# A graph network layer stack on one core: two looped slots in the adjacency build, and four basis chunks moved to the ends of tiles 9 and 11 of the first layer

## Time and profile before

| | us |
|---|---|
| median of 3 runs | 1826.44 (1819.98 to 1828.72) |
| the profiled execution | 1818.69 |
| its span, first to last instruction | 1816.4 |
| TensorE busy | 1754.4 (97%) |
| VectorE busy | 874.3 (48%) |
| ScalarE busy | 593.8 (33%) |
| build, about | 22 to 321 us of the span |
| first layer, tiles 0 to 11 | about 454 to 596 us |

### The profile page before, as it was taken

How to read it: one execution, slowest core, us unless ns; L and a number is a source line. 1 busy time by engine, 2 the same in 40 slices (tenths; PEclk the granted TensorE clock), 3 DMA queues, 4 the chain that set the end, 5 groups by cost and what they waited for, 6 DMA issues and landing times.

```text
span 1816.4 us, 22290 instructions
## 1 busy us (share of the span) xinstructions
PE 1754.4 (97%) x7318; PEld 849.3 (47%) x7318; DVE 874.3 (48%) x1889; ACT 593.8 (33%) x1232; POOL 10.8 (1%) x36
## 2 busy tenths in 40 slices
PE   5989888999999999999999999999999999999998
PEld 3555555433334444444444444444544444444444
DVE  7888887489885321112222224334253443594123
ACT  1555544466876311222110001232323323232000
POOL 1000000000000000000000000000000000000000
PEclk9999999999999999999999999999999999999999
DMA  7999989810302401000011116300000010021111
GB/s 176 247 288 280 247 235 245 318 36 2 144 24 82 168 4 43 0 1 23 0 47 35 35 35 241 147 0 30 1 0 30 1 41 1 1 82 58 35 47 47
DMA packets 45781, 157.80 MB, mean 87 GB/s; under 512 B 7686, under 2 KB 9630, under 8 KB 37094
## 3 DMA queue, kind: packets, MB, share of 16 engines
q1 hardware_dynamic: 43792, 146.95, 26.6%
q10 hardware_dynamic: 1878, 9.44, 1.4%
HBM read 120.71 MB, written 35.65 MB: 86 GB/s over the span
## 4 chain that ended last, share of the span: by engine, by line
PE 83%; DVE 6%; DMA 5%; issue 3%; DVEq 2%; ACT 1%; POOL 0%; POOLq 0%; ACTq 0%
PE psum L1549 31%; PE psum L1563 31%; PE psum L1790 7%; DMA hs<-in_L_gnn_basis 4%; PE psum L1477 2%; PE psum L1444 2%; PE psum L1740 2%; PE psum L1637 2%; PE psum L1624 1%; PE psum L1476 1%; PE psum L1515 1%; DMA adj<-in_L_gnn_basis 1%; DVE hs L716 1%; DVEq L695 1%; PE psum L1716 1%
## 5 line engine op out<-in xcount | busy, mean ns | idle before, releaser
L1563 PE MATMUL psum<-hs,adj 128*128 128x512 f16 x2880 | 636.3, 380 | 0.0
L1549 PE MATMUL psum<-wb,xt 128*128 128x512 f32 x1056 | 457.7, 593 | 0.0
L1563 PEld LDWEIGHTS psum<-hs,adj 128*128 128x128 f16 x2880 | 281.2, 98 | 330.6 <-issue 11.0
L1549 PEld LDWEIGHTS psum<-wb,xt 128*128 128x128 f32 x1056 | 199.2, 190 | 244.8 <-issue 243.2
L1328 ACT ACTIVATE ua<-ua 128x512 f32<-128x512 f32 x60 | 37.8, 629 | 314.9 <-DVE ua L1106 181.2
L1102 DVE SCALAR_TENSOR_TENSOR vt<-psum,scl,xt 128x512 f32<-128x512 f32 x60 | 44.8, 746 | 192.7 <-PE psum L1563 192.7
L1037 DVE TENSOR_TENSOR vt<-psum,adj 128x512 f32<-128x512 f32 x24 | 16.6, 692 | 249.0 <-PE psum L1549 249.0
L1549 PE MATMUL psum<-adj,xt 128*128 128x512 f32 x288 | 130.1, 595 | 0.0
L1790 PE MATMUL psum<-hs,adj 128*128 128x512 f32 (+1 forms) x312 | 123.8, 560 | 0.0
L1477 PE MATMUL psum<-hs 128*128 128x192 f32 x404 | 99.7, 329 | 0.0
L1316 ACT ACTIVATE lnst<-lnst,bcol 128x1 f32<-128x1 f32 x24 | 7.1, 295 | 280.1 <-DVE lnst L1015 270.6
(11 more groups left out here) (249 smaller groups left out, 1741.5 us busy)
## 6 DMA issues: line engine op xcount, KB each, us to landing
hs<-in_L_gnn_basis SPq DMA_DIRECT2D x38, 960.0 KB, 12.9
adj<-in_L_gnn_basis SPq DMA_DIRECT2D x26, 960.0 KB, 14.5
aw_scratch<-xt ACTq DMA_DIRECT2D x12, 768.0 KB, 10.4
adj<-aw_scratch SPq DMA_DIRECT2D x1, 9216.0 KB, 36.8
x_scratch<-adj SPq DMA_DIRECT2D x24, 256.0 KB, 2.3
hs<-x_scratch SPq DMA_DIRECT2D x24, 256.0 KB, 2.6
ts_scratch<-adj SPq DMA_DIRECT2D x2, 2304.0 KB, 19.0
as_scratch<-adj SPq DMA_DIRECT2D x1, 4608.0 KB, 16.8
```

What stands on the lines that cost most here:

```text
L1549: x = pe.matmul(psum[:, bank, :], xt[:, i, k, :], w[:, k, :], start=first and k == 0, stop=last and k == 3)
L1563: x = pe.matmul(psum[:, i % 2 + (4 * half if own else 0), :], adj[:, m, j, P * i:P * i + P], hs[:, t, half, j, :], start=n == 1 or (own an ...
```

## The change

Five things are done together:

1. A sixth slot (`looped_t`, a tensor of its own). The looped steps of even windows use slot 4, those of odd windows slot 5; the slot is fixed for all steps of one window. The scan of the step counts becomes two scans, over even and odd windows.
2. 60 chunks stay in the build, spread evenly over windows 1 to 94 (`IN_BUILD`), and the limit from which two buffers are left goes from 52 to 48.
3. The other four, chunks 14, 15, 30 and 31 of `basis2`, are mixed by `late_pair(0)` and `late_pair(1)` at the ends of tiles 9 and 11 of the first layer, behind that tile's `rows` and image matmul and ahead of BACK_LAST.
4. ScalarE's queue loads them: two chunks when the sums of squares are done, two more within `late_copy(0)`. ScalarE copies each mixed pair (`late_copy`, ahead of the copies of tiles 3 and 9), and SP stores it (`late_stores`, behind the stores of tiles 4 and 11). The buffers lie where the tanh worked, so ScalarE now waits for `halves_used` and the squares go elsewhere.
5. SP's order: the gate rows are loaded before x tile 9 instead of after it; `late_stores(0)` stands before the load of x tile 11.

```diff
-SLOTS = 5
+SLOTS = 6
+        looped_t = sb("looped", [P, P + W * NT + W * NT], F32)
-        squares_in = adj_flat[2][:, 0:2 * D].bitcast(BF16)...
+        squares_in = adj_flat[2][:, 16 * D:18 * D].bitcast(BF16)...
+        late_basis = [part(adj_flat[2], 8192 * k, [4 * D]) for k in range(2)]
+        late_mixed = part(adj_flat[2], 16384, [D])
-        FAR_CHUNKS = 52
+        LATE = 4
+        LATE_AT = {9: 0, 11: 1}
+        LATE_COPY = {3: 0, 9: 1}
+        IN_BUILD = 64 - LATE
+        FAR_CHUNKS = 48
+        def looped_slot(w):
+            return 4 + w % 2
-            if u % 3 != 2:
-                n = 2 * (u // 3) + u % 3
+            if u < NW - 1 and (u + 1) * IN_BUILD // (NW - 1) > u * IN_BUILD // (NW - 1):
+                n = u * IN_BUILD // (NW - 1)
                 here.append(("basis", n // (CH // 2), n % (CH // 2)))
...
# SP
+            def late_stores(p):
+                sp.wait_ge(late_read, p + 1)
+                for q in range(4):
+                    sp.dma_start(combs[1][q, (CH - LATE) % (CH // 2) // 2 + p, :, :], late_mixed[32 * q:32 * q + 16, :]).then_inc(late_out, 16)
-            for i in range(2, 10):
+            for i in range(2, 9):
                 first_load(i)
             sp.wait_ge(halves_used, LOTS)
             gate_load(0)
+            first_load(9)
             first_store(0)
             first_store(1)
             first_load(10)
             for i in range(2, 5):
                 first_store(i)
+            late_stores(0)
             first_load(11)
...
             for i in range(9, NT):
                 first_store(i)
+            late_stores(LATE // 2 - 1)
+            sp.wait_ge(late_out, 64 * (LATE // 2))
# VectorE
-            step(dve.tensor_tensor_scan(wrow[0:1, 2, :], wrow[0:1, 1, :], wrow[0:1, 1, :], 0.0, ALU.add, ALU.bypass))
+            by_turn = wrow[0:1, :, :].rearrange("p a (w t) -> p a t w", t=2)
+            for t in range(2):
+                x = dve.tensor_tensor_scan(by_turn[:, 2, t, :], by_turn[:, 1, t, :], by_turn[:, 1, t, :], 0.0, ALU.add, ALU.bypass)
+            step(x)
                 with dve.Fori(0, steps) as q:
-                    dve.wait_ge(onehot_free[LOOPED], before + q + 1)
+                    dve.wait_ge(onehot_free[looped_slot(w)], before + q + 1)
...
# ScalarE
             act.wait_ge(halves_ready, LOTS)
+            act.wait_ge(halves_used, LOTS)
...
+            act.wait_ge(sq_ready, n_sq[0])
+            def late_loads(p):
+                for k in range(2):
+                    c = (CH - LATE) % (CH // 2) // 2 + p + 16 * k
+                    act.dma_start(late_basis[k][0:120, :], bases[1][:, c * (4 * D):(c + 1) * (4 * D)]).then_inc(late_in[k], 16)
+            late_loads(0)
+            def late_copy(p):
+                act.wait_ge(late_ps, 2 * p + 2)
+                if p < LATE // 2 - 1:
+                    late_loads(p + 1)
+                if p:
+                    act.wait_ge(late_out, 64 * p)
+                act.activation(late_mixed, psum[:, 2 + p % 2, :], ACT.Copy).then_inc(late_read, 1)
...
                 if i:
                     j = i - 1
+                    if j in LATE_COPY:
+                        late_copy(LATE_COPY[j])
                     act.wait_ge(t_ps, tick(0, j))
# TensorE
+            def late_pair(p):
+                for h in range(2):
+                    pe.wait_ge(late_in[h], 16 * (p + 1))
+                    for v in range(4):
+                        x = pe.matmul(psum[32 * v:32 * v + 32, 2 + p % 2, :], attw[0:120, 1, 1 - h:33 - h], late_basis[h][0:120, D * v:D * v + D], start=h == 0, stop=h == 1, skip_group_check=True)
+                    x.then_inc(late_ps, 1)
                 dots()
+                if i in LATE_AT:
+                    late_pair(LATE_AT[i])
                 for j in BACK_LAST.get(i, ()):
                     turned_back(j)
+                if (r, i) == (1, 0):
+                    pe.wait_ge(late_read, LATE // 2)
```

More of the change, by code:

```diff
@@ L193, in follower @@
         def follower(n):
-            return min([m for m in range(n + 1, 64) if basis_of(m) == basis_of(n)], default=None)
+            return min([m for m in range(n + 1, IN_BUILD) if basis_of(m) == basis_of(n)], default=None)
         aw_stage = xt[:, :, :, :].rearrange("p a b d -> p (a b d)")[:, 0:2 * NT * P].rearrange("p (k j d) -> p k j d", k=2, j=NT)
@@ L209, in program @@
         pairs.append(rest[:, N + 256:N + 256 + 2 * SLOT].rearrange("p (k x) -> p k x", k=2))
-        onehots_at = [pairs[0][:, 0, :], pairs[0][:, 1, :], pairs[1][:, 0, :], pairs[1][:, 1, :], looped]
+        onehots_at = [pairs[0][:, 0, :], pairs[0][:, 1, :], pairs[1][:, 0, :], pairs[1][:, 1, :], looped, looped_t[:, :]]
         onehot_s = [v[:, 0:P] for v in onehots_at]
@@ L282, in program @@
         act_done = sem("act_done")
+        late_in = [sem(f"late_in{k}") for k in range(2)]
+        late_ps, late_read, late_out = sem("late_ps"), sem("late_read"), sem("late_out")
         attw_ready, att_all, picked = sem("attw_ready"), sem("att_all_ps"), sem("pick_ready")
@@ L400, in x_load @@
                 sp.dma_start(x_first[:, a:b, :], ins["x"][P * a:P * b, :].rearrange("(k p) d -> p k d", p=P)).then_inc(x_in[g], 16)
-            for n in range(CH):
+            for n in range(IN_BUILD):
                 l, c = n // (CH // 2), n % (CH // 2)
@@ L509, in _ @@
                 first_store(i)
+            late_stores(0)
             first_load(11)
-            for i in range(5, 9):
+            first_store(5)
+            for i in range(6, 9):
                 first_store(i)
@@ L733, in _ @@
                 with dve.Fori(0, steps) as q:
-                    dve.wait_ge(onehot_free[LOOPED], before + q + 1)
+                    dve.wait_ge(onehot_free[looped_slot(w)], before + q + 1)
                     last = nc.s_assert_within(first + q + 2, 0, EC - 1, skip_runtime_bounds_check_because=why)
-                    source(LOOPED, last)
-                    keys(LOOPED, last, n, u)
+                    source(looped_slot(w), last)
+                    keys(looped_slot(w), last, n, u)
                 if w + 1 < NW:
@@ L1488, in _ @@
                 with pe.Fori(0, steps) as q:
-                    pe.wait_ge(onehot_ready[LOOPED], before + q + 1)
-                    counts(b, LOOPED, False)
+                    pe.wait_ge(onehot_ready[looped_slot(w)], before + q + 1)
+                    counts(b, looped_slot(w), False)
                 for lot in by_window[w]:
@@ L1692, in _ @@
             softmax_back(0)
+            def late_pair(p):
+                if p >= 2:
+                    pe.wait_ge(late_read, p - 1)
+                for h in range(2):
[3 more added lines that the diff above has]
+                    x.then_inc(late_ps, 1)
             def turned_back(j):
```

9 lines of the change are left out of this document (4 added, 5 removed).

## The result

| us | kernel before | kernel after |
|---|---|---|
| median | 1822.45 (10 runs, 1814.05 to 1828.72) | 1833.05 (10 runs, 1829.41 to 1835.56) |
| the profiled execution | 1818.69 | 1833.95 |
| its span | 1816.4 | 1832.1 |
| mean granted TensorE clock | 1.000 | 0.996 |

The ratio is 1.0056, with a 95% interval of 1.0043 to 1.0069: 10.2 us slower (0.0056 x 1822), where the forecast was 2.6 us slower. From 1822.45 the forecast would have been 1825, 8 us too low. The size of the change was missed by a factor of four.

A forecast was written before the change was run, and what follows sets the result against it. The prediction took VectorE to bound the build and TensorE the first layer's last tiles. Build -3.6 and first layer +6.2 sum to +2.6 us, giving a median of 1829 us; main case 1822 to 1835, outer numbers 1815 and 1838.

The forecast's parts named there:

- So VectorE sets the build: Build: VectorE sets the pace at 2.61 us a window; TensorE needs less, 2.5 us a window on average.
- the two faster rivals: Build: TensorE sets it (-24 us, some 1809, chance 0.07), or the chunk loads do (-18 us, 1815, chance 0.07).
- Build -3.6: Build: slot waits -0.6, second scan +0.2, lags -1.9, last windows -1.3 us; bounds 0 and -13.
- The lags: Build, nine two-step windows up to 84: TensorE's lag behind VectorE falls from 5.5 to 3.6 us, -1.9.
- First projection 3 to 4 us earlier: Sign in the new profile, behind the build: the first projection starts 3 to 4 us earlier than 329.9.
- Late matmuls +4.0: First layer: two pairs of two chunks, 4 x 0.99 us, where TensorE has no idle time.
- Late issue +0.8: First layer: ScalarE issues two loads ahead of the table load, on the chain to the first turn; +0.8 us.
- Late loads in time, 0: First layer: the first two loads land at 573.5 us, just in time; 0, upper bound 5 us.
- What the loads do to the stores: First layer, tile 2: store 0 lands 4.9 us later, so TensorE waits for the row; +1.3 us (0 to 5).
- Tile 10: First layer: tile 7 waits for store 5; its path of 11.6 us is against TensorE's own time; +0.1 us (0 to 5).
- The slower rival: First layer, tiles 9 to 11: late loads starve it, stores land late, +14.7 us over three tiles; 1842 us, chance 0.16.
- gaps in tiles 9 to 11 exceed 4 us: First layer: sign that the forecast is wrong, TensorE gaps of over 4 us in these tiles.

The follow-up runs named there:

- experiment 3: Kernel after with its four late loads cut from 2048 to 32 columns, all instructions kept: ratio 1.0007 to the kernel before, 1822.89 us.
- experiment 4: Kernel after with the first two late loads issued earlier, ahead of the softmax: ratio 1.0042 to the kernel before, 1828.11 us.
- experiment 5: Kernel after with the late loads on SyncE's queue, behind stores 0 and 1 and behind store 6: ratio 1.0021 to the kernel before, 1824.58 us.
- experiment 6: Kernel after, late loads still on ScalarE's queue but issued once stores 0 and 1, then store 6, have landed: ratio 1.0021 to the kernel before, 1826.83 us.
- experiment 7: Kernel after with its 60 build chunks in the windows the kernel before used for them, last in window 88: ratio 1.0072 to the kernel before, 1833.98 us.
- experiment 8: Kernel after with old chunk windows, first late loads early, second pair loaded by SP and mixed in the next layer: ratio 1.0016 to before, 1823.95 us.
- experiment 9: Kernel after with its new chunk windows, first late loads early, second pair loaded by SP and mixed in the next layer: ratio 1.0014 to before, 1823.01 us.
- experiment 2: Kernel after without late pairs, their loads, copies and stores; stand-in stores at the build's end: ratio 1.0007 to the kernel before, 1823.38 us.
- experiment 1: Kernel before with only the sixth slot and the two scans: ratio 0.9997 to the kernel before, 1820.93 us.
- experiment 10: All 64 chunks in the build, two ahead of window 0, last four windows free, two looped slots, no late part: ratio 1.0009 to the kernel before, 1824.84 us.

## Why the prediction was right and wrong

The build's worth by the medians is the ratio times 1822, less what the first layer's stages of the same kernel's profile are longer (14.0 us for the kernel after; 4.8, 8.5, 5.6, 8.4, 12.0, 3.9 and 3.9 for experiments 3 to 9, the last two with the 2.05 of the next layer; and the 4.8 of experiment 2).

| build against before, us | |
|---|---|
| new windows: after, experiments 2, 3, 4, 5, 6, 9 | -3.8, -3.5, -3.5, -0.8, -1.8, -4.6, -1.4: mean -2.8 |
| old windows: experiments 7, 8 | +1.1, -1.0 |
| slots alone: experiment 1 | -0.5 |

Each has an uncertainty of some 2 to 3 us from its own interval, so only the mean is used. It rests on the medians: in the profiles the first projection starts at 327.2 to 332.5 with the new windows (330.1 in the mean of six, experiment 2 apart), as it does before (329.92), but that execution was 4 us under its median.

- **"So VectorE sets the build": held.** Four chunks fewer on TensorE gave some 3 us, against 18 and 24 of the two faster rivals. The claim was too narrow, though: the chunk loads are a second bound right behind it. With all 64 chunks asked for two places sooner, TensorE waits 20.5 us for them in experiment 10.
- **Build -3.6: about right** (mean -2.8). The lags, read window by window in VectorE's timeline, came out as forecast where nothing else interfered: in the first eight two-step windows its waits are 1.36, 1.07, 1.38, 2.07, 1.36, 0.99, 1.18 and 0.99, 10.4 us in all. The eight forecast lags and eight round trips of 0.82 are 10.0, and the kernel before has 12.0. The ninth, window 84, broke the sum: 5.6 us instead of 1.0, so that all ten are 18.2 and not 14 to 15. That is chunk 52, for which I had no term: the limit of two buffers moved from chunk 52 to 48, and chunk 52 takes a round trip of 10.0 us just ahead of a two-step window. At the end, the load that was to gain 1.3 us gained 0.8 (7.78 instead of 8.54). So part of the agreement of the total is luck.
- **First projection 3 to 4 us earlier: not so in the profile** (1.3 later). Stretches of 3.41 us at half clock from 122.0 and from 275.6 on are in it, and none is in the profiled execution of before, which was 4 us under its median.
- **Ten waits of 1.03 and round trips of 8 to 10 at the end: both there.**
- **Late matmuls +4.0:** measured 3.7. **Late issue +0.8:** measured 1.05.
- **Late loads in time, 0:** right in the kernel after; the pair of 579.57 finds its chunks landed at 571.7. The forecast of 573.5 was near.
- **"What the loads do to the stores" and "Tile 10", +1.3 and +0.1: this is the term that was mis-sized, and it stands in both.** Measured 2.89 and 3.13. I took a store beside the loads to be 4.9 us slower than 2.0, so 6.9, from ScalarE's stores in the build. In this stretch a store lands just behind the load that was issued ahead of it: 8.4 us for store 0 and 9.6 for store 5. For tile 2 the 1.5 us more make +1.3 into 2.8. For tile 7 the path was the forecast one, from the end of the pair over the copies, row 5 and store 5 to row 7; it took 14.7 us instead of 11.6, 2.7 of them in the store. `late_stores(0)`, which the forecast names, held store 5 up by nothing: it was issued at 585.61, when row 5 was done at 585.58. The forecast put TensorE's own time in that tile at the same 11.6 us, so nothing was left to absorb a longer store.
- **The clock: no term at all.** 1.45 + 1.74 = 3.2 us, a consequence of the two waits. With it, the waits cost 4.3 and 4.9 us.
- **The slower rival** had the right mechanism and too high a price: 6.0 us of waits and 3.2 of clock, in two tiles, against its 14.7 in three. The mark "gaps in tiles 9 to 11 exceed 4 us" was met, 5.7 in the sum of the two.

So the first layer costs 14.0 us instead of 6.2, and the build gives 2.8 by the mean instead of 3.6: 11.2 by these two, 10.2 measured. In the prediction I cited the Trainium skill, DMA: Bandwidth & Descriptors, "Issuing engines are not separate DMA queues"; experiments 5 and 6 agree with it. The same page of the Trainium skill has in "Queues, rings and completion order" the statement that I should have weighed: a transfer's semaphore increment is a write that lands only after every earlier write of that DMA engine, across its queues. Experiments 3 and 6 show the effect, landings of 2.0 us once the bytes or the order are changed; that this rule is its cause, rather than the mere sharing of the DMA engines, no run here separates.

None of the eleven kernels beats the kernel before by more than its interval. Two pairs cost 3.7 to 3.9 us where TensorE is busy and the build returns about 3, so a late part of this form loses about a microsecond even without a stall.

## What to carry to other kernels

When large loads are put beside small stores, first list whose buffer is released by a store issued **behind** them; issue the stores first, or the loads where no such store follows within their landing time. Work moved from an engine that isn't the bound of its stage to a stage where it is costs its full length there and returns only what the waits allow. And a wait of 2.7 to 3.0 us on TensorE brought the lower clock level each of the five times that it arose in the first layer: price it with that.

## What the runs showed of the hardware

- A store of 256 KB that takes 2.0 us alone took 7.8 to 9.6 us behind two loads of 960 KB on another queue that still moved (kernel after), and landed 0.5 to 1.6 us after the second of them; 8.3 and 10.1 us in experiment 6. Behind such loads on its own queue it took up to 9.7 (experiment 5).
- In the first layer the waits of TensorE of 2.69, 2.72, 2.74, 2.88 and 2.97 us (the kernel after and experiments 4, 6 and 7) all had a stretch of 3.41 us at the 1.2 GHz level that began between 0.5 us before their end and 1.0 us behind it. Of three waits of 1.60 us (the kernel after and experiments 3 and 7) one had it (experiment 7), and the one of 1.69 (experiment 5) didn't. In the build such a stretch also came 1.5 us behind a wait of 1.03 us (at 122.0 in the kernel after), while waits of 2.66 (at 314.7 in the kernel after) and 2.71 us (at 276.5 in experiment 4) brought none, so the length of one wait doesn't decide it there. Each stretch in the first layer cost 1.5 to 1.7 us.
- Two DMA issues on ScalarE in front of a table load cost 1.05 us, where the issue rows say 2 x 0.33; the first of the two took 0.61.
